# Neighbour codes moved to the one-hots' side by DMA transposes, with a new order of steps, in a two-layer graph kernel

## The chip, the cores and the metric

One NeuronCore of a Trainium2 chip. The metric is the device time of one execution in microseconds (us), as the median of several runs. The engines are TensorE (PE; its weight loads are shown as PEld), VectorE (DVE), ScalarE (ACT) and GpSimd (POOL); SyncE (SP) issues most of the DMAs and does no arithmetic. Each engine has one in-order queue of its own, and the five meet only through semaphores.

## What is computed

```
B, N, C, H = 16, 1024, 64, 128          # x [16,1024,64], adj [16,1024,1024]
h = max(layernorm(x), 0)
x = x + (adj / clip(rowsum(adj), 1)) @ h                          # layer 0
h = max(layernorm(x), 0)
neigh = (adj > 0) off the diagonal;  rank = running count of neighbours in a row
skip  = ceil(n_neighbours / 2) if n_neighbours > 10 else 1
rem   = neighbours whose rank % skip == skip - 1, made symmetric  # thinned out
nd    = what is left, and the node itself
agg[n, c] = 0.25 q25 + 0.5 q50 + 0.25 q75 over h[nd(n), c]        # interpolated quantiles
out = x + (relu((h + agg) @ W1 + b1) @ W2 + b2) * mask
```

The quantiles are the hard part: each node and channel needs a sorted list of its neighbours' values.

## The kernel before, in words

The 16 graphs ("batches") are worked off in 8 pairs, g = 0 to 7, b = 0 and 1.

**Preparation, one batch after another.** For each of 8 row tiles (128 rows) SP loads `ADJ` and, in two halves, its transpose `ADJT`. PE forms the layer-0 messages from `ADJT` (L481). ACT turns `ADJ` into 0/1 neighbours `NEI` (L741, L743), POOL clears the diagonal (`no_loops`, L1270), DVE scans them into running counts in `VR` (`count`, L1045, which first waits until the previous batch's scatter has read that tile of `VR`). POOL works out the thinning of four tiles at a time (L1283 to L1304), ACT and DVE mark the removed neighbours in `RM` (L750, L1051), PE adds up the codes in PSUM (L502 to L511), ACT brings them back as one code per pair of nodes (`coded`, L774) and counts them (`valid`, L779). ACT also ranks the nodes by number of neighbours (L759). POOL then scatters each tile's rows to DRAM, to the place of their rank (`scatter`, L1328). A row of `rows` is 1024 codes, then the node's normalised values h1, x1 and a few counts.

**Lists, one pair at a time.** In rank order the nodes fall into four blocks, `b1` (384 nodes, from 128), `hub` (the 128 with most neighbours), `b2a` (256) and `b2b` (256). The one-hots need the codes with the neighbour on the partitions, so they are transposed: for each of the 16 tiles of a pair SP loads 128 ranked rows into `RR` (L456; two buffers), PE transposes eight 128x128 squares into one of the two PSUM banks `psT` (`positions_up`, L519), ACT copies them to `POSA` or `POSB` (`positions_down`, L790). The tile's h1 is turned too (`turn`, L526) and copied to `Z` (L798). DVE compares `POS` with slot numbers (`one_hots`, L1065, L1068), PE multiplies the one-hots with h1 (`gather`, L560, 14 chunks in two halves), ACT takes the lists out (L861, L866), DVE sorts them (L1086, L1091 for the two smaller kinds; L1132, L1133 with ACT's L884 for the hub), weighs them with coefficients (L1109, L1102, L1138) and adds up (L1150). Two small products, a turn back (L614, L621, L631), the mask (L1157) and POOL's addition (L1354) give the output, which POOL scatters back to node order, 8 indirect DMAs for each of the two batches (`put`, L1362).

**Order.** All steps are laid out in one list, and each engine walks through it taking its own. The list comes from `strands()` (steps of one kind in sequence, one letter each) and `plan()`, which reads the string `ORDER` once for each pair; a letter takes the next step of its strand. `SKEW` says how many steps each strand is ahead: adjacency tiles (`A`, with 16 in a pair) run 24 ahead, that is one and a half pairs. Letters used below: A adjacency tile (ACT, POOL, SP), D scan, T thinning, B and r the removed ones, s and c codes and their count, S scatter of rows, L load of ranked rows, F the transposes through PSUM, d one-hots, m gather, t hub merge (DVE), Q coefficient and weighing, v the two turns of the counts on PE and V the step of POOL ahead of them, E end of a pair, O output scatters. The lead-in before pair 0 can start its one-hots is the same string with the letters of strands that have not begun skipped (`LEAD = 4` passes).

The lines quoted fix the old path's waits: a bank of `psT`, and an area of `POS` that is free when its last gather is done.

```
def positions_up(g, b, rt):                                   # PE
    w.wait_ge(d_row[n % 2], 16 * (n // 2 + 1))
    o = t_free("pos", g, b, rt).bitcast(F16)
    for k in range(T):
        m = e.transpose(o[:, k * P:k * P + P], RR[:, n % 2, k * P:k * P + P], idh)
def positions_down(g, b, rt):                                 # ACT
    w.wait_ge(t_full, u + 1)
    w.wait_ge(p_gm, GATHERED[before])
```

Of the kernel before, what the change touches and what calls it, by code (L numbers as in the profile page):

```python
# [8 lines left out]
ACT = mybir.ActivationFunctionType  # L9
# [15 lines left out]
LEAD = 4  # L25


ORDER = (
    "mRJAssMtQQcNtfJtsQdtFMJtmQtQtdtANetdtQNQQQkmmMMQQdSdQQmQSQaQQmQQcQeLdAMMsFcmssQfQSFSALMdQcDDLMsesSAcdRmS"
    "FMMAVessMMDDTmcSAsQEsDcEdhVSmvFKDMMKdABEBKvdBBmMDMDTdKeFEmRBmeoBEKErBldmrgNFBdKLdrrmFEmrNdeekmdmKdedXEmr"  # L30
    "NrrmeLnQKFstnscssFKAnMsFtMcSsKLFtLScSssdAMtQsscDMdtsDcsSFEAtmMSLMcsAsMSdMEDtEcssSRcSFFADmMMFFtQTtLdFALMM"
    "FmmAeLQFDFQLtdOMMBFFAmFFDBDQQtLdMLFeFmhBrDrFQTMtQtrlBLFFFQQetQrLdBBBBdrtgrrrGOQtmmFsJsGtdctQJsset")

SKEW = {
# [102 lines left out]
def strands():  # L137

    s = {c: [] for c in SKEW}

# [55 lines left out]
    def finish(g):  # L196
# [8 lines left out]
        for b in range(2):  # L205
            add("O", "out", g, b)

    for g in range(NP):
# [3 lines left out]
        for b in range(2):  # L212
            prepare(g, b)
        for blk in BLOCKS:
            fill(g, blk)
# [18 lines left out]
def plan():  # L234

    pl = Plan()
    pl.do("start")
    steps = strands()
    at = {c: SKEW[c] - LEAD * len(steps[c]) // NP for c in SKEW}
    for c in ORDER * (NP + 2 * LEAD):  # L240
        if 0 <= at[c] < len(steps[c]):
            kind, *a = steps[c][at[c]]
            if kind in ("pos", "turn", "dg", "sc", "nvt", "nvr", "flg", "f1", "f2"):
# [38 lines left out]
def program(nc, x_d, adj_d, adjt_d, mask_d, w1_d, b1_d, w2_d, b2_d, cf_d, ch_d, ci_d, cr_d, sel_d, tile_d, row_d, h1_d, out_d):  # L282
    with ExitStack() as ctx:
# [17 lines left out]
        RR = sb("RR", [P, 2, R_X1], F16)  # L301
# [40 lines left out]
        def feat(v, at, w=1):  # L342
# [6 lines left out]
        d_adj, d_adjt, d_row, d_out, d_feat = (  # L349
            [sem(f"{n}{i}") for i in range(2)] for n in ("d_adj", "d_adjt", "d_row", "d_out", "d_feat"))  # L350
# [46 lines left out]
        def positions(g, blk, half):  # L397
# [4 lines left out]
        def turned(g, blk):  # L402
            return positions(g, blk, 0)

        def sync(e):
            w = Once(e)
            for kind, *a in steps:
# [40 lines left out]
                elif kind == "ldr":  # L448
                    g, b, rt = a
                    n = nth["ldr", g, b, rt]  # L450
                    for t in range(T):
                        w.wait_ge(d_sca[t], 16 * (2 * g + b + 1))
                    if n >= 2:
                        w.wait_ge(t_full, t_use("turn", *filled[n - 2]) + 1)
                    n0 = (2 * g + b) * N + rt * P
                    e.dma_start(RR[:, n % 2].bitcast(I32), row_d[n0:n0 + P, 0:R_X1 // 2]).then_inc(d_row[n % 2], 16)  # L456
# [3 lines left out]

        filled = [tuple(s[1:]) for s in steps if s[0] == "ldr"]

        def tensor(e):
# [50 lines left out]
            def positions_up(g, b, rt):  # L514
                n = nth["ldr", g, b, rt]
                w.wait_ge(d_row[n % 2], 16 * (n // 2 + 1))
                o = t_free("pos", g, b, rt).bitcast(F16)
                for k in range(T):
                    m = e.transpose(o[:, k * P:k * P + P], RR[:, n % 2, k * P:k * P + P], idh)  # L519
                m.then_inc(t_full, 1)  # L520
# [960 lines left out]
```

## Time and profile before

| | |
|---|---|
| time, median of 3 runs | 1654.02 us (1653.05 to 1656.76) |
| the profiled execution | 1666.68 us, its span 1664.6 us |
| busy: DVE, PE, ACT, POOL | 1375.1, 1270.5, 1227.5, 775.7 us |
| instructions | 29516 |
| DMA | 233.99 MB, mean 141 GB/s |
| mean granted TensorE clock | 0.878 |

"Busy" is time in which an instruction ran; the rest of the span is the engine's idle time. An idle stretch is put down to what ended it, the releaser. Times are microseconds from the span's start unless marked ns. An engine that is busy for most of a stretch sets its length, and what can still be won there is its idle time.

### The profile page before, as it was taken

How to read it: one execution, taken by the hardware profiler on the slowest of the kernel's cores; microseconds unless marked ns; L12 is line 12 of the kernel's file. 1: busy time of each engine (PE TensorE's matmuls, PEld its weight loads, DVE VectorE, ACT ScalarE, POOL GpSimd, SP SyncE). 2: the span in 40 equal slices, each digit the busy share in tenths (PEclk: the TensorE clock that was granted, in tenths of full speed). 3: DMA queues.
4: the chain of work that ended last, by engine and by line, in shares of the span. 5: the costliest groups of instructions: out<-in, count | busy, mean ns of one | idle time of the engine just before them, and what ended most of it. 6: DMA issues, size and time to landing. Idle time of an engine off the chain costs nothing. (4 is left out here: it accounts for less than half of the span.)

```text
span 1664.6 us, 29516 instructions
## 1 busy us (share of the span) xinstructions
PE 1270.5 (76%) x10929; PEld 847.7 (51%) x10929; DVE 1375.1 (83%) x2557; ACT 1227.5 (74%) x2099; POOL 775.7 (47%) x996
## 2 busy tenths in 40 slices
PE   4675897879888788878888788869888797768642
PEld 3553664556546564556546464556546564444320
DVE  3444459999899898989899898989899898969990
ACT  3687797988788797968788788868788787833310
POOL 0252425271628643383728643383616744631344
PEclk9966598999898898979898998979798898979775
DMA  5464754463536362554536363454526462330100
GB/s 157 139 208 133 235 189 138 149 205 118 171 106 219 113 219 88 172 167 136 182 104 220 112 216 94 163 164 131 197 82 224 124 210 67 109 82 23 30 12 13
DMA packets 139386, 233.99 MB, mean 141 GB/s; under 512 B 62910, under 2 KB 63438, under 8 KB 139224
## 3 DMA queue, kind: packets, MB, share of 16 engines
q1 hardware_dynamic: 124888, 185.54, 36.4%
q0 software_dynamic: 14336, 46.42, 7.4%
q8 instruction: 86, 1.41, 0.4%
q14 instruction: 76, 0.62, 0.1%
HBM read 181.31 MB, written 50.59 MB: 139 GB/s over the span
## 5 line engine op out<-in xcount | busy, mean ns | idle before, releaser
L560 PE MATMUL psG<-OHB,HL 128*64 128x384 f16 (+5 forms) x3584 | 387.4, 361 | 55.1 <-DVE OHB L1065 34.8
L1045 DVE TENSOR_TENSOR_SCAN VR<-NEI 128x1024 f16<-128x1024 f16 x128 | 296.8, 2336 | 125.0 <-POOL NEI L1270 57.3
L481 PE MATMUL psL<-H0A,ADJT 128*128 128x65 f32 x2048 | 311.9, 311 | 65.1 <-DMA ADJT<-in_adjt 37.3
L481 PEld LDWEIGHTS psL<-H0A,ADJT 128*128 128x128 f32 x2048 | 294.7, 224 | 101.7 <-DMA ADJT<-in_adjt 61.2
L560 PEld LDWEIGHTS psG<-OHB,HL 128*64 128x64 f16 x3584 | 213.0, 117 | 195.7 <-DVE OHB L1065 54.0
L1270 POOL TENSOR_TENSOR NEI<-NEI,CH 128x128 f16<-128x128 f16 x128 | 114.1, 894 | 295.8 <-ACT NEI L743 294.5
L1328 POOL DMA_INDIRECT rows<-VR,IDX x128 | 185.4, 1449 | 57.9 <-ACT NEI L779 34.4
L774 ACT ACTIVATE VR<-psT,CF 128x512 f16<-128x512 f32 x256 | 168.5, 681 | 24.6 <-PE psT L511 22.4
L1132 DVE TENSOR_TENSOR HUB<-HUB 128x1472 f32<-128x1472 f32 (+6 forms) x224 | 178.4, 796 | 8.1 <-ACT HUB L884 7.9
L1133 DVE TENSOR_TENSOR HUB<-HUB 128x1472 f32<-128x1472 f32 (+6 forms) x224 | 184.8, 825 | 0.0
L1362 POOL DMA_INDIRECT out<-FR x128 | 162.1, 1266 | 37.5 <-issue 36.9
L884 ACT ACTIVATE HUB<-HUB 128x1472 f32<-128x1472 f32 (+5 forms) x168 | 89.5, 533 | 100.1 <-DVE HUB L1133 98.5
L741 ACT ACTIVATE NEI<-ADJ 128x1024 f16<-128x1024 f32 x128 | 135.1, 1055 | 32.8 <-DMA ADJ<-in_adj 29.6
L750 ACT ACTIVATE RM<-VR,SK 128x1024 f16<-128x1024 f16 x128 | 142.5, 1147 | 16.9 <-POOL SK L1304 16.7
L1065 DVE TENSOR_SCALAR OHB<-POSB 128x512 f16<-128x512 f16 (+2 forms) x544 | 133.0, 313 | 22.9 <-PE psG L560 20.6
L502 PE MATMUL psT<-VR,CH 128*128 128x512 f16 x256 | 104.9, 410 | 59.7 <-ACT VR L774 17.1
L606 PE MATMUL psM<-W,CF 128*128 128x384 f32 (+4 forms) x192 | 84.0, 556 | 78.9 <-DVE W L1109 77.2
L759 ACT ACTIVATE JUNK<-psT,SK 128x1024 int8<-128x1024 f32 x128 | 140.6, 1147 | 0.0
L743 ACT ACTIVATE NEI<-NEI 128x1024 f16<-128x1024 f16 x128 | 135.3, 1057 | 4.1
L779 ACT ACTIVATE NEI<-VR 128x1024 f16<-128x1024 f16 x128 | 135.0, 1055 | 1.3
L1065 DVE TENSOR_SCALAR OHB<-POSA 128x1536 f16<-128x1536 f16 (+6 forms) x320 | 118.2, 427 | 6.6 <-PE psG L560 5.4
L508 PEld LDWEIGHTS psT<-CH,RM 128*128 128x128 f16 x1024 | 86.9, 103 | 64.9 <-issue 14.5
(120 smaller groups left out, 2260.9 us busy)
## 6 DMA issues: line engine op xcount, KB each, us to landing
ADJ<-in_adj SPq DMA_DIRECT2D x128, 512.0 KB
ADJT<-in_adjt SPq DMA_DIRECT2D x256, 256.0 KB
RR<-rows SPq DMA_DIRECT2D x128, 288.0 KB
FR<-rows SPq DMA_DIRECT2D x16, 272.0 KB, 4.0
X<-in_x SPq DMA_DIRECT2D x16, 256.0 KB, 3.5
h<-VR SPq DMA_DIRECT2D x16, 256.0 KB
rows<-VR,IDX POOLq DMA_INDIRECT x128
out<-FR POOLq DMA_INDIRECT x128
```

The lines of the kernel that those rows point to most:

```text
L481: m = e.matmul(ps["L"][:, 65 * (t % 4):65 * (t % 4) + 65], ADJT[:, hf, j, :], H0A[:, T * b + k, :], start=(k == 0), stop=(k == T - 1), ski ...
L560: m = e.matmul(bk[C * b:C * b + C, 0:cols], HL[:, part, (2 * g + b) % 3, k, :], OHB[:, n % 2, b, kk * cols:kk * cols + cols], start=(k == ...
L743: e.activation(nei, nei, ACT.Relu).then_inc(a_nei, 1)
L750: e.activation(RM[:, t, :], VR[:, t, 0:N], ACT.Abs, bias=SK[:, 3, t:t + 1]).then_inc(a_abs, 1)
L759: m = e.activation(JUNK[:, t % 2, :], psT[:, :, :].rearrange("p i c -> p (i c)"), ACT.Sign, bias=SK[:, 5, t:t + 1], accum_out=RS[:, t:t + 1])
L774: e.activation(VR[:, k, 512 * ch:512 * ch + 512], t_bank(u), ACT.Relu, bias=CF[:, CF_LOW:CF_LOW + 1]).then_inc(t_empty, 1)
L1045: e.tensor_tensor_scan(VR[:, t, 0:N], NEI[:, t, 2:N + 2], NEI[:, t, 1:N + 1], 0.0, ALU.add, ALU.add).then_inc(v_cum, 1)
L1065: last = e.tensor_scalar(oh[:, :, at:at + nn], pos, float(2 * d0 - 1), None, ALU.is_equal)
L1132: e.tensor_tensor(b0, a0, a1, ALU.max)
L1133: e.tensor_tensor(b1, a0, a1, ALU.min).then_inc(v_bat, 1)
L1328: e.indirect_dma_start(row_d[:, :], bass.IndirectOffsetOnAxis(ap=IDX[:, gb % 2, t:t + 1], axis=0), VR[:, t, :].bitcast(I32), None).then_in ...
L1362: e.indirect_dma_start(out_d, bass.IndirectOffsetOnAxis(ap=dst, axis=0), fr[:, rt, 0:2 * C].bitcast(F32), None).then_inc(d_out[g % 2], 16)
```

## The change

The path through PE and ACT is taken out for the codes (`positions_up`, `positions_down`, 128 steps each, and `RR`). In its place SP issues one DMA transpose for each block and batch (`ldr`, 64 in all) from DRAM to `POSA` or `POSB`. It waits for the 8 scatters of its batch and until the one-hots that last read this area are made (`v_oh`). Since `RR` also brought h1, a new load `ldh` (letter H, 16 in all) brings h1 of a whole batch to `HR`; `turn` reads it there. DVE's one-hots wait for the DMA's semaphore. `ORDER` is a new string; the lead-in has a string of its own, `LEAD_IN`; strands in it start at 0, others `LATE` steps behind. `put` covers half of the rows of both batches instead of all rows of one.

```diff
-LEAD = 4
 ORDER = (
+    "tJetsscdJstsRQJAmtssQtQdtJtJOOctsmMMNQeHtQAtdNtdtQkQQmmeQcQQQMdHmLQNQffQaQSdQQQQdmMSAMmssQQcMFdSmAVsMhFF"
+    "FFeeQSdcMDDDFdDRSAmsTsMMQcAsKKEdsScKSMMLAssmmDlcDDBMVMdSKAEdBmeBvmvDKTeddoBKMMEmBmBEKedLgBmRdFBErreFrNdk"
+    "QmtmKNddmrmrrrrdNKesesssXnscEtsnKntSsAmFdMMQtsLdctcmdAMEStmSMLEsedADtDcMsMEcAMssMEtSSEscmRtsscADdMtsGMAQ"
+    "QcSFMMetmFSFFQADSQQDQtMMDALQtTQFmQtDDhMTBQBtLBBBlrtdeFtQrrdGBBBrFrLmrMmQrrg")
+LEAD_IN = (
+    "XnnnAMMAMMAMMAMMADDDDTRMMAMBBDBMAMMDADMDTrBBMrBrBrBRNrrrrgNsscsscsAssMcsMAkMMAMNMscSsSAMssMcsDSScRsSADMM"
+    "SADDcTsSsMMAcDSMMADDhDBBrlTBBMMrrBBrRBNrrgXBNNrrknsnscnssAMMScsscAMsSMsADcLMssSMADssScMSMARDDDsscSMMAcDs"
+    "TsMcSMSAMMDBADrBrBBhTLBrrBBBlMMgddrrLrrmm")
+LATE = {"E": 11, "J": 5, "O": 4, "Q": 24, "a": 1, "t": 12}
...
     def fill(g, blk):
+        for b in range(2):
+            add("L", "ldr", g, b, blk)
         for rt in range(r0 // P, (r0 + width) // P):
             for b in range(2):
-                add("L", "ldr", g, b, rt)
-                add("F", "pos", g, b, rt)
                 add("F", "turn", g, b, rt)
...
-        for b in range(2):
-            add("O", "out", g, b)
+        for ch in range(2):
+            add("O", "out", g, ch)
...
-    at = {c: SKEW[c] - LEAD * len(steps[c]) // NP for c in SKEW}
-    for c in ORDER * (NP + 2 * LEAD):
+    at = {c: 0 if c in LEAD_IN else -LATE.get(c, 0) for c in steps}
+    for c in LEAD_IN + ORDER * (NP + 2):
...
+        MADE = {(g, blk): 1 + max(nth["gd", g, c, 1] for c in OF[blk]) for g in range(NP) for blk in OF}
+        LAST = {"b1": (1, "b2a"), "hub": (1, "b2b"), "b2a": (0, "b1"), "b2b": (0, "hub")}
...
+                elif kind == "ldh":
+                    g, b = a
+                    for t in range(T):
+                        w.wait_ge(d_sca[t], 16 * (2 * g + b + 1))
+                    if g:
+                        w.wait_ge(t_full, t_use("turn", g - 1, b, T - 1) + 1)
+                        w.wait_ge(d_hr[b], 16 * g)
+                    n0 = (2 * g + b) * N
+                    e.dma_start(HR[:, b].bitcast(I32), row_d[n0:n0 + N, R_H1 // 2:R_X1 // 2].rearrange(
+                        "(t p) f -> p t f", p=P)).then_inc(d_hr[b], 16)
                 elif kind == "ldr":
+                    g, b, blk = a
+                    area, r0, width = BLOCKS[blk]
                     for t in range(T):
                         w.wait_ge(d_sca[t], 16 * (2 * g + b + 1))
+                    back, last = LAST[blk]
+                    if g >= back:
+                        w.wait_ge(v_oh, MADE[g - back, last])
+                    if g:
+                        w.wait_ge(d_pos[blk][b], 16 * g)
+                    n0 = (2 * g + b) * N + r0
+                    e.dma_start(POS[area][:, b, :, 0:width], row_d.bitcast(F16)[n0:n0 + width, 0:N],
+                                transpose=True).then_inc(d_pos[blk][b], 16)
...
             def turn(g, b, rt):
+                w.wait_ge(d_hr[b], 16 * (g + 1))
                 o = t_free("turn", g, b, rt)
+                e.matmul(o[C * b:C * b + C, 0:P], HR[:, b, rt, :].bitcast(F32), idf, start=True, stop=True).then_inc(
+                    t_full, 1)
...
                     for piece, d0, nd, nn in CHUNKS[c]:
-                        w.wait_ge(t_empty, positions(g, piece, half))
+                        w.wait_ge(d_pos[piece][b], 16 * (g + 1))
...
-            def put(g, b):
-                fr = FR[:, (2 * g + b) % 4]
-                w.wait_ge(o_fin, 2 * (g + 1))
-                for rt in range(T):
+            def put(g, ch):
+                w.wait_ge(o_fin, 2 * g + ch + 1)
+                for b, rt in itertools.product(range(2), range(4 * ch, 4 * ch + 4)):
+                    fr = FR[:, (2 * g + b) % 4]
```

## Rows read from the trace of the kernel before

**Rows 1.** The page, busy time, share of the span and instructions of each engine.

```profile
PE 1270.5 (76%) x10929; PEld 847.7 (51%) x10929; DVE 1375.1 (83%) x2557; ACT 1227.5 (74%) x2099; POOL 775.7 (47%) x996
```

**Rows 2.** Stretches: length, busy PE, PEld, DVE, ACT, POOL; clock, DMA share, GB/s.

```profile
0.00:204.00 204.00, 125.94 (x704) 99.71 (x704) 85.35 (x90) 140.03 (x191) 70.18 (x141) 0.79 0.54 171
204.00:379.00 175.00, 140.99 (x1215) 95.62 (x1216) 147.84 (x266) 149.75 (x245) 75.60 (x106) 0.92 0.54 174
379.00:1319.00 940.00, 771.83 (x6841) 514.96 (x6838) 860.96 (x1597) 764.03 (x1312) 491.79 (x617) 0.90 0.48 154
1319.00:1598.00 279.00, 212.14 (x2021) 128.60 (x2018) 257.16 (x551) 166.87 (x336) 116.82 (x112) 0.91 0.27 83
1598.00:1665.00 67.00, 19.57 (x154) 8.79 (x154) 23.76 (x56) 6.86 (x17) 21.31 (x21) 0.60 0.03 11
```

**Rows 3.** Waits of DVE from 291 to 1458 us: total, times, longest.

```profile
DVE VR L1045 <- POOL NEI L1270: 28.0, 13, 4.8
DVE OHB L1065 <- PE psG L560: 20.1, 6, 4.2
DVE VR L1045 <- issue: 13.9, 4, 4.8
```

**Rows 4.** Timeline near 1100 us, POOL and DVE: start, length, idle before.

```profile
1101.54 2.89 POOL L1362 DMA_INDIRECT out<-FR  x1 [0.16 <-issue]
...
1113.90 0.96 POOL L1362 DMA_INDIRECT out<-FR  x1 [0.30 <-issue]
1114.88 0.45 POOL L1270 TENSOR_TENSOR NEI<-NEI,CH 128x128 f16<-128x128 f16 x1
...
1115.36 2.29 DVE L1045 TENSOR_TENSOR_SCAN VR<-NEI 128x1024 f16<-128x1024 f16 x1 [4.76 <-issue]
```

**Rows 5.** Timeline near 1010 us, PE and DVE.

```profile
1006.17 0.28 PE L530 MATMUL psT<-CF,NV 128*16 128x128 f32 x1 [3.72 <-POOL NV L1336]
...
1016.20 1.71 DVE L1065 TENSOR_SCALAR OHB<-POSB 128x512 f16<-128x512 f16 x8 [3.40 <-PE psG L560]
```

**Rows 6.** Groups by line: busy us, mean ns, idle before.

```profile
L1045 DVE TENSOR_TENSOR_SCAN VR<-NEI 128x1024 f16<-128x1024 f16 x128 | 296.8, 2336 | 125.0 <-POOL NEI L1270 57.3 <-DMA rows<-VR,IDX 53.9 <-issue 13.9
L1133 DVE TENSOR_TENSOR HUB<-HUB 128x1472 f32<-128x1472 f32 (+6 forms) x224 | 184.8, 825 | 0.0
L1132 DVE TENSOR_TENSOR HUB<-HUB 128x1472 f32<-128x1472 f32 (+6 forms) x224 | 178.4, 796 | 8.1 <-ACT HUB L884 7.9
L519 PE MATMUL psT<-CH,RR 128*128 128x128 f16 x1024 | 88.7, 237 | 26.2 <-ACT POSA L790 10.9 <-DMA RR<-rows 4.8 <-ACT VR L774 4.4
L790 ACT ACTIVATE POSA<-psT 128x1024 f16<-128x1024 f16 x80 | 81.8, 1023 | 30.4 <-PE psT L519 21.8 <-PE psT L526 3.7 <-remote 2.6
L790 ACT ACTIVATE POSB<-psT 128x1024 f16<-128x1024 f16 x48 | 48.8, 1017 | 35.3 <-PE psT L519 28.6 <-PE psT L511 6.4
```

**Rows 7.** Around the first one-hot: ACT, POOL, ACT, DVE.

```profile
176.92 1.06 ACT L779 ACTIVATE NEI<-VR 128x1024 f16<-128x1024 f16 x1
178.34 0.98 POOL L1328 DMA_INDIRECT rows<-VR,IDX  x1 [2.11 <-ACT NEI L779]
188.25 1.00 ACT L790 ACTIVATE POSA<-psT 128x1024 f16<-128x1024 f16 x1
204.02 1.96 DVE L1065 TENSOR_SCALAR OHB<-POSA 128x1536 f16<-128x1536 f16 x4 [1.25 <-ACT Z L798]
```

**Rows 8.** DMA issues: KB each, median us from issue to landing.

```profile
FR<-rows SPq DMA_DIRECT2D x16, 272.0 KB, 4.0
X<-in_x SPq DMA_DIRECT2D x16, 256.0 KB, 3.5
```

**Rows 9.** Waits of SP's queue.

```profile
SPq L456 <- PE psT L526: 512.4, 81, 16.1
```

**Rows 10.** End of the run on POOL: the last addition, the last of 16 scatters.

```profile
1637.60 1.26 POOL L1354 TENSOR_TENSOR FR<-FR,HID 128x512 f32<-128x512 f32 x1 [0.23 <-DVE HID L1157]
...
1658.10 0.96 POOL L1362 DMA_INDIRECT out<-FR  x1 [0.30 <-issue]
```

More of the change, by code:

```diff
@@ L137, in strands @@
 def strands():
-    s = {c: [] for c in SKEW}
+    s = {c: [] for c in ORDER}
     def add(c, kind, *args):
@@ L213, in strands @@
             prepare(g, b)
+        for b in range(2):
+            add("H", "ldh", g, b)
         for blk in BLOCKS:
@@ L238, in plan @@
     steps = strands()
-    at = {c: SKEW[c] - LEAD * len(steps[c]) // NP for c in SKEW}
-    for c in ORDER * (NP + 2 * LEAD):
+    at = {c: 0 if c in LEAD_IN else -LATE.get(c, 0) for c in steps}
+    for c in LEAD_IN + ORDER * (NP + 2):
         if 0 <= at[c] < len(steps[c]):
             kind, *a = steps[c][at[c]]
-            if kind in ("pos", "turn", "dg", "sc", "nvt", "nvr", "flg", "f1", "f2"):
+            if kind in ("turn", "dg", "sc", "nvt", "nvr", "flg", "f1", "f2"):
                 pl.use("T", kind, *a)
@@ L348, in program @@
         d_sca = [sem(f"d_sca{t}") for t in range(T)]
-        d_adj, d_adjt, d_row, d_out, d_feat = (
-            [sem(f"{n}{i}") for i in range(2)] for n in ("d_adj", "d_adjt", "d_row", "d_out", "d_feat"))
+        d_adj, d_adjt, d_hr, d_out, d_feat = (
+            [sem(f"{n}{i}") for i in range(2)] for n in ("d_adj", "d_adjt", "d_hr", "d_out", "d_feat"))
+        d_pos = {blk: [sem(f"d_pos_{blk}{i}") for i in range(2)] for blk in BLOCKS}
         CONST = 13 * 16
@@ L395, in m_left, with turned @@
             return {"wz": v_wz, "mk": v_fa}[step[0]], nth[step] + 1
[L397 removed]
+        def turned(g, blk):
             _, r0, width = BLOCKS[blk]
             return max(t_use("turn", g, b, rt) for b in range(2) for rt in range(r0 // P, (r0 + width) // P)) + 1
[L402 to L403 removed]
+        MADE = {(g, blk): 1 + max(nth["gd", g, c, 1] for c in OF[blk]) for g in range(NP) for blk in OF}
+        LAST = {"b1": (1, "b2a"), "hub": (1, "b2b"), "b2a": (0, "b1"), "b2b": (0, "hub")}
         def sync(e):
@@ L459, in sync @@
             w.wait_ge(d_h1, 16 * B)
-        filled = [tuple(s[1:]) for s in steps if s[0] == "ldr"]
         def tensor(e):
@@ L512, in codes @@
                          skip_group_check=True).then_inc(t_full, 1)
[L514 to L520, printed above, removed]
             def turn(g, b, rt):
-                n = nth["ldr", g, b, rt]
+                w.wait_ge(d_hr[b], 16 * (g + 1))
                 o = t_free("turn", g, b, rt)
-                h1 = RR[:, n % 2, R_H1:R_H1 + 2 * C].bitcast(F32)
-                e.matmul(o[C * b:C * b + C, 0:P], h1, idf, start=True, stop=True).then_inc(t_full, 1)
+                e.matmul(o[C * b:C * b + C, 0:P], HR[:, b, rt, :].bitcast(F32), idf, start=True, stop=True).then_inc(
+                    t_full, 1)
             def valid_up(g):
@@ L780, in valid @@
                              accum_out=feat(VR, R_NV)[:, k, :]).then_inc(a_cn, 1)
-            def positions_down(g, b, rt):
-                u = t_use("pos", g, b, rt)
-                blk, = [n for n, (_, r0, width) in BLOCKS.items() if r0 <= rt * P < r0 + width]
-                area, r0, _ = BLOCKS[blk]
-                before = {"b1": (g - 1, "b2a"), "hub": (g - 1, "b2b"), "b2a": (g, "b1"), "b2b": (g, "hub")}[blk]
-                w.wait_ge(t_full, u + 1)
-                if before[0] >= 0:
-                    w.wait_ge(p_gm, GATHERED[before])
-                e.activation(POS[area][:, b, :, rt * P - r0:rt * P - r0 + P],
-                             t_bank(u).bitcast(F16).rearrange("p (k n) -> p k n", n=P), ACT.Copy).then_inc(t_empty, 1)
             def turned_down(g, b, rt):
```

19 lines of the change are left out of this document (2 added, 17 removed), and 3 rows, old and new, of the table SKEW.

## The prediction

> **What bounds the kernel now.** Read the busy times first [rows 1]: DVE is busy 1375.1 us of 1664.6, 83%, ACT and PE some 75%. The average hides the stages, so I cut the span at three landmarks [rows 2]: the first one-hot at 204 us, the first pair's `b1` sum at 379 us, the same sum of the sixth pair at 1319 us, and then the run-out.
> - 0 to 204: DVE is busy 85 of 204 us. Nothing is full. Two batches have to go one after the other through load, scan, removal, codes, scatter, and the first one-hots need both.
> - 379 to 1319: five periods of 188.0 us. DVE is busy 860.96 us, 172.2 a period, so 15.8 us of each are idle. DVE is the bound at 92%; ACT has 152.8 us of work a period and PE 154.4, busy by the modelled ends.
> - 204 to 379: DVE idle 27 us of 175. 1319 to 1598: idle 22 of 279. After 1598: idle 43 of 67, a serial chain.
>
> So work taken off ACT and PE pays nothing by itself in a period. It pays only if one of DVE's 15.8 idle microseconds goes, and no more than these can go: this change leaves all of DVE's instructions in place. The third view is what ended DVE's idle times in the steady part [rows 3]: 28.0 us behind POOL's diagonal clearing, 13.9 us "issue" ahead of the same scan, 20.1 us behind a gather on PE. The timeline explains the two longest kinds. Near 1115 us DVE stands 4.76 us ahead of a scan, because POOL clears the diagonal for it only at 1114.88, and from 1101.54 on POOL has been issuing eight output scatters [rows 4]; the first ones took up to 2.89 us. That pause of 4.75 to 4.76 us is once in every period. Near 1016 us DVE waits 3.40 us for a gather; PE had stood 3.72 us ahead of the counts' turn (L530), which waits for POOL, with the gather queued behind it [rows 5]. That one comes six times, 3.4 us on average.
>
> **The change, part by part.**
> *Codes' old path.* 128 steps with 8 transposes each on PE, 88.7 us of busy time, 11.1 a pair. On ACT 80 + 48 copies, 81.8 + 48.8 = 130.6 us, 16.3 a pair [rows 6]. Both lie beside DVE's work in a period; I cost their removal at nothing there, with DVE's 172.2 as the cover. It gives slack: ACT falls to 136.5 us of 188. It also gives back 16 uses a pair of the two `psT` banks.
>
> *Waits of DVE in a period.* In the old string the first `O` (8 scatters) stands one adjacency tile ahead of a `D`: O M M B F F A m F F D. In the new one both O's stand together, and until the next `D` there are seven one-hot steps (about 1 us each, [rows 7]), five merges (1.62 each, [rows 6]) and a score of Q letters, over 20 us of DVE work. The eight scatters took 13.3 us, 1.67 each [rows 4]; 16 take 20 to 27. I take the 4.75 us out whole. The counts' turn: old V S m v, new V and then t d v v, with the V's themselves further from the loads `f`. I take the 3.4 us out whole as well. Together -8.1 a period. Against this, two O's in one piece hold POOL for that long, in which rows of the batch in preparation can't be scattered and `R`'s additions can't be made. A new pause of at least 1 us seems certain in an order this tight: +1. Net -7 a period, bounds -15.8 (every idle time gone) and +4 (the block meets a scan). Five periods: -35.
>
> *The transposes.* 64 DMAs, 768 KB for b1, 256 KB for the hub, 512 KB for each of b2a and b2b, 33.6 MB in all, where `RR` carried 37.7 MB, and 16 loads of h1 with 4.2 MB: the bytes are equal. No row shows the rate of a DMA transpose. Nearest rows: plain loads with rows of 256 or 272 bytes, 256 KB in 3.5 us and 272 KB in 4.0 us from issue to landing [rows 8], at most 68 to 73 GB/s; and the 174 GB/s that all queues moved together in a stretch [rows 2]. The two b1 transposes of a pair, 1.5 MB, take 9 us at the one and 22 at the other. I take about 13, nearer the stretch, since the loads of rows 8 are mostly the fixed part of a short DMA. The cover: between a pair's last scatter and its first one-hot the new string has four scans (9.3 us), five merges of 1.62 (8.1) and small steps of some 3 us, 20 us of DVE work [rows 6]. With 2 to 3 us until the scatter has landed the b1 transposes end after 16, hidden by 4; at 22 us they would be late by 5 in each pair. b2a and b2b have the six hub chunks as cover. Cost taken: 0; bounds 0 and +5 a pair.
>
> The Trainium skill speaks against the choice of queue: "Advanced Engine Details and Errata", section DGE: Hardware vs Software, lists transposes as worse by the hardware generator, which SP uses, than by the software one. The same page's X-Bar Transpose section has them as fast as plain DMAs, by which nothing in the sum changes. No row here shows either; the first is the rival below.
>
> *SP's queue.* The old loads held it 512.4 us in all for a free `RR` [rows 9], with `ADJ` and `ADJT` queued behind. That wait goes. The new ones are for the scatters, as before, and for one-hots already made, 64 times instead of 128. Behind a transpose stand `A` loads (two buffers) and `H`. Gain: none in a period, where DVE rules; in the lead-in it is part of the next item. If SP needs long to issue a transpose, the next `ADJT` is late: bound +3 a pair.
>
> *Lead-in.* The last code count of pair 0 begins at 176.92 and its scatter at 178.34; the first copy to POSA is at 188.25 and the first one-hot at 204.02 [rows 7]. Those 25.7 us hold six round trips through PSUM, beside scans and removals of batch 2. In the new string 5 B, 5 r, T, one `D` and a tile stand there, 10 to 12 us of work, and the transposes need 2.5 + 13: about 17 us. That is -9. Six or seven copies of 1.02 us go from ACT, whose 140 us in 204 are the most of any engine in this stretch [rows 2]: -6 at most, and I take it. Sum -15, bounds -30 and +5 (the order of the rest is new, and the codes of batch 1 may come later).
>
> *Between.* 204 to 379, idle 27 us: one period's -7, since its output-free POOL gave no 4.75 us pause but much idle behind scatters. 1319 to 1598: the gather pause once, little preparation left: -3. The run-out: 16 scatters of 1.26 us follow the last addition [rows 10]. `put` by halves could begin after the first half's addition, but both O's still stand behind both halves' E steps, and the chain is as long as before: 0.
>
> *Sum.* -15 - 7 - 35 - 3 = -60 against the profiled execution of 1666.68 us: 1606.7. The median is 12.7 us lower than that execution, so 1654.0 - 60 = 1594. **Forecast 1596 us**, about 3.5% less, with 2 us for pauses that I can't name.
>
> **The rivals.**
> (a) *The pauses only move.* The lead-in gains, but DVE still stands 15 us in a period behind other releasers, as it did with an order that had seemed tight. 1654 - 15 - 5 = 1634. For it: 13 of the scans waited for POOL, and POOL's work doesn't shrink. Against: the two repeated pauses have causes that the new string parts.
> (b) *DVE runs full.* The idle time falls to 4 a period: -12 x 5 - 15 - 14 = -89, 1565. For it: ACT and PE now have 50 us of slack each.
> (c) *Slower: b1's transposes land late.* The place is the first one-hot of every pair. The cover is 20 us. If the 1.57 MB take more than 17.5 us (90 GB/s; 2.5 us are the scatter's) DVE waits. The sign turns where that costs 60 / 8 = 7.5 us a pair, at 25 us or 63 GB/s. Half of rows 8's 70 GB/s is 45 us: 27.5 too long, x 8 = 220, less the 60, 1814. A middle case of 35 us gives 1654 - 60 + 8 x 17.5 = 1734, which I take as its time. The skill's "worse" would be this. For it: no row shows the rate, and short rows land slowly. Against: the DMA engines are busy only 0.48 of the time [rows 2].
> (d) *The change moves nothing:* gains of the lead-in are eaten by late transposes. 1654.
>
> **How the numbers follow.** Forecast's case (1580 to 1612) 0.42, (a) 0.20, (b) 0.13, (d) 0.05, (c) 0.20. The range 1560 to 1672 leaves out the far part of (c), 0.13, and the tip of (b). The likeliest case's own range is 1580 to 1612. This kernel's runs spread so that a difference under 0.2% (3 us) can't be told from none. Faster 0.77, the same 0.04, slower 0.19.
>
> **What would show it.** Right: no idle time of 4.7 us ahead of a scan behind output scatters; no 3 to 4 us ahead of one-hots behind the counts' turn; DVE idle under 10 us a period; the first one-hot at or before 190 us; ACT busy near 1097 us, DVE near 1375. Wrong: one-hots that wait for a DMA into POSA, a sign of (c); PE waiting longer for `ADJT`, a sign that transposes hold SP or the DMA engines; periods of 185 us or more, (a). A transposing DMA that also slowed all other traffic would make the whole forecast wrong.

## The result, and the profile after

The changed kernel takes 1789.95 us in the median of 4 runs (1777.02 to 1793.14), against 1654.18 us for the kernel before on the same chip: a ratio of 1.081, interval [1.0761, 1.086]. The forecast was 1596 us. The profiled execution has a span of 1775.2 us against 1664.6: the medians are 135.8 us apart, the two spans 110.6, since the profiled execution of the kernel before was 12.5 us above its median and this one 12.9 us below. The stages below divide up the 110.6.

First the page of the changed kernel, busy time, share and instructions, beside [rows 1]:

```profile
PE 1255.8 (71%) x9905; PEld 811.1 (46%) x9905; DVE 1382.1 (78%) x2557; ACT 1107.8 (62%) x1971; POOL 770.8 (43%) x996
```

The work changed as the prediction had it (ACT 1107.8 us, forecast 1097; DVE 1382.1, forecast 1375). What grew is idle time, DVE's above all. The same stages, cut at the first one-hot and at the `b1` sums of the first, sixth and seventh pair; columns as in [rows 2]:

```profile
0.00:202.00 202.00, 112.33 (x643) 89.99 (x643) 84.86 (x91) 132.21 (x179) 64.31 (x131) 0.82 0.55 170
202.00:392.00 190.00, 141.25 (x1058) 91.20 (x1058) 144.85 (x262) 132.34 (x228) 81.11 (x117) 0.81 0.55 156
392.00:1417.00 1025.00, 764.09 (x6190) 492.53 (x6190) 867.25 (x1596) 688.56 (x1231) 481.13 (x604) 0.83 0.51 142
1417.00:1590.00 173.00, 135.28 (x1126) 83.22 (x1128) 149.74 (x303) 116.08 (x227) 85.89 (x95) 0.87 0.43 116
1590.00:1775.00 185.00, 102.86 (x892) 54.14 (x888) 135.38 (x311) 38.64 (x109) 58.34 (x51) 0.74 0.11 25
```

The first `b1` sum comes 13 us later (392.2 against 379.2). Five periods take 1025 us, 205.0 each, against 187.9: 85 us. The seventh pair adds 9 us and the rest 3; together the 110.6 us between the spans. In a period DVE has 867.25 / 5 = 173.5 us of work (before 172.2) and 31.6 us of idle time (before 15.8). So the loss is idle time of DVE in the steady part, and the next view says what ended it. Waits in that stretch, engine, line, tile, releaser, then total, times and longest; the counterpart is [rows 3]:

```profile
DVE VR L1038 <- DMA rows<-VR,IDX: 45.9, 18, 5.5
DVE OHB L1058 <- PE psG L568: 34.6, 6, 8.4
DVE HUB L1125 <- ACT HUB L879: 31.1, 22, 3.1
DVE OHB L1058 <- issue: 18.2, 4, 5.7
DVE RM L1044 <- ACT RM L756: 9.9, 5, 2.3
DVE OHB L1061 <- PE psG L568: 4.4, 2, 2.8
DVE MARK L1213 <- issue: 4.1, 1, 4.1
...
DVE VR L1038 <- POOL NEI L1263: 0.5, 2, 0.2
...
ACT NEI L747 <- DMA ADJ<-in_adj: 54.1, 10, 9.5
ACT RM L756 <- POOL SK L1297: 50.5, 14, 7.6
...
SPq L269 <- DMA out<-FR: 55.4, 4, 14.0
```

The same view of the kernel before, from 379 to 1319:

```profile
DVE VR L1045 <- POOL NEI L1270: 25.0, 10, 4.8
DVE OHB L1065 <- PE psG L560: 15.9, 5, 4.0
DVE VR L1045 <- DMA rows<-VR,IDX: 10.3, 11, 1.9
...
DVE HUB L1132 <- ACT HUB L884: 2.8, 3, 1.0
...
SPq L267 <- DMA out<-FR: 57.5, 4, 15.5
```

The marks (RM) had 0.6 us there. The pause of [rows 4], scans behind POOL's clearing, did go, as predicted. Five others came or grew in its place. None is a wait for `POSA` or `POSB`: the transposes landed in time.

The fourth of the list has no releaser ("issue"). It stands once in every period where DVE comes to a branch: `overflow` loads a flag, tests it and then writes `MARK` (L1213). First the changed kernel, then the kernel before:

```profile
873.93 0.30 DVE L1058 TENSOR_SCALAR OHB<-POSB 128x512 f16<-128x512 f16 x1 [5.71 <-issue]
...
992.95 0.06 DVE L1220 MEMSET MARK<- 128x1 f32 x1
```

In the five periods these pauses are 18.2 + 4.1 = 22.3 us. In the kernel before no `MARK` of the steady part has a pause ahead of it; there two long scans and the hub's addition stand just ahead of the branch, in the changed kernel short comparisons. That the scans cover the branch is my reading, not shown by a run of its own.

One period's largest pause, of 8.37 us, shows how such a chain is followed. The timeline of the changed kernel, start, length, engine and, in brackets, the idle time before; first the `b1` sums that bound the steady part:

```profile
392.17 0.55 DVE L1143 SCALAR_TENSOR_TENSOR Z<-Z,psM 128x384 f32<-128x384 f32 x1
...
810.99 1.16 POOL L1355 DMA_INDIRECT out<-FR  x1 [0.16 <-issue]
...
831.63 0.96 POOL L1355 DMA_INDIRECT out<-FR  x1 [0.30 <-issue]
...
833.83 1.02 SPq L450 DMA_DIRECT2D FR<-rows  x2
834.89 0.83 SPq L432 DMA_DIRECT2D ADJ<-in_adj  x1
...
840.79 1.06 ACT L747 ACTIVATE NEI<-ADJ 128x1024 f16<-128x1024 f32 x1 [8.93 <-DMA ADJ<-in_adj]
...
841.91 1.97 PE L497 MATMUL psL<-H0A,ADJT 128*128 128x65 f32 x8 [10.25 <-DMA ADJT<-in_adjt]
843.81 2.66 PE L568 MATMUL psG<-OHB,HL 128*64 128x368 f16 x16
...
846.52 1.71 DVE L1058 TENSOR_SCALAR OHB<-POSB 128x512 f16<-128x512 f16 x8 [8.37 <-PE psG L568]
...
1417.24 0.55 DVE L1143 SCALAR_TENSOR_TENSOR Z<-Z,psM 128x384 f32<-128x384 f32 x1
```

POOL issues 16 output scatters in one block, 20.6 us from the first to the last. SP comes to the loads `f` (`FR`, L450), which overwrite rows that output scatters read, and stands until 833.83. `ADJ` and `ADJT` for the preparation are behind it in SP's queue. PE comes to a message step without its `ADJT` and stands 10.25 us with a gather queued behind (L568), and the gather is what DVE's one-hots wait for. The page puts DVE's idle time down to PE; the cause lies further back, in SP's queue and, behind that, in the scatters. The stop itself isn't new: in five periods SP stood 57.5 us for output scatters before and 55.4 us now. New is that the loads behind it come too late: PE waited 15.0 us for `ADJT` before and 51.3 us now.

### The profile page after: what moved, and what is told of

The parts are those of the page before. It is cut to its first block and busy times, and to the rows that moved or that the text cites. A ratio compares the mean times of both kernels' runs of the same rounds, so it can differ in the third digit from the quotient of the medians.

```text
span 1775.2 us, 27210 instructions
## 1 busy us (share of the span) xinstructions
PE 1255.8 (71%) x9905; PEld 811.1 (46%) x9905; DVE 1382.1 (78%) x2557; ACT 1107.8 (62%) x1971; POOL 770.8 (43%) x996
## 5 line engine op out<-in xcount | busy, mean ns | idle before, releaser
L568 PE MATMUL psG<-OHB,HL 128*64 128x384 f16 (+5 forms) x3584 | 424.2, 386 | 76.4 <-DVE OHB L1058 60.9
L497 PE MATMUL psL<-H0A,ADJT 128*128 128x65 f32 x2048 | 319.2, 313 | 139.2 <-DMA ADJT<-in_adjt 92.7
L497 PEld LDWEIGHTS psL<-H0A,ADJT 128*128 128x128 f32 x2048 | 300.8, 226 | 175.3 <-DMA ADJT<-in_adjt 103.8
L568 PEld LDWEIGHTS psG<-OHB,HL 128*64 128x64 f16 x3584 | 224.9, 125 | 239.0 <-DVE OHB L1058 77.5
L1263 POOL TENSOR_TENSOR NEI<-NEI,CH 128x128 f16<-128x128 f16 x128 | 125.9, 983 | 363.1 <-ACT NEI L749 362.2
L1321 POOL DMA_INDIRECT rows<-VR,IDX x128 | 181.1, 1415 | 95.0 <-ACT NEI L785 68.4
L1355 POOL DMA_INDIRECT out<-FR x128 | 137.8, 1077 | 38.0 <-issue 37.7
L614 PE MATMUL psM<-W,CF 128*128 128x384 f32 (+4 forms) x192 | 89.1, 585 | 79.5 <-DVE W L1102 79.5
L518 PE MATMUL psT<-VR,CH 128*128 128x512 f16 x256 | 108.8, 425 | 42.4 <-ACT VR L780 21.9
L1058 DVE TENSOR_SCALAR OHB<-POSA 128x1536 f16<-128x1536 f16 (+6 forms) x320 | 122.5, 437 | 4.2 <-PE psG L568 4.2
```

The lines of the kernel that those rows point to most:

```text
L497: m = e.matmul(ps["L"][:, 65 * (t % 4):65 * (t % 4) + 65], ADJT[:, hf, j, :], H0A[:, T * b + k, :], start=(k == 0), stop=(k == T - 1), ski ...
L568: m = e.matmul(bk[C * b:C * b + C, 0:cols], HL[:, part, (2 * g + b) % 3, k, :], OHB[:, n % 2, b, kk * cols:kk * cols + cols], start=(k == ...
L1058: last = e.tensor_scalar(oh[:, :, at:at + nn], pos, float(2 * d0 - 1), None, ALU.is_equal)
L1321: e.indirect_dma_start(row_d[:, :], bass.IndirectOffsetOnAxis(ap=IDX[:, gb % 2, t:t + 1], axis=0), VR[:, t, :].bitcast(I32), None).then_in ...
L1355: e.indirect_dma_start(out_d, bass.IndirectOffsetOnAxis(ap=dst, axis=0), fr[:, rt, 0:2 * C].bitcast(F32), None).then_inc(d_out[g % 2], 16)
```

## The experiments

Theories at the start: T1, the transposes cost it (they hold SP's queue or slow the other DMAs); T2, the new order of steps costs it.

**1. Plain loads in place of the transposes.** The new order, the same bytes, no transposing:

```diff
-                    e.dma_start(POS[area][:, b, :, 0:width], row_d.bitcast(F16)[n0:n0 + width, 0:N],
-                                transpose=True).then_inc(d_pos[blk][b], 16)
+                    for r in range(width // P):
+                        src = row_d[n0 + r * P:n0 + r * P + P, 0:N // 2].rearrange("p (k f) -> p k f", k=T)
+                        e.dma_start(POS[area][:, b, :, r * P:r * P + P].bitcast(I32), src).then_inc(
+                            d_pos[blk][b], 16)
```

> The changed kernel with each DMA transpose replaced by plain loads of the same rows into the same area, in pieces of 256 bytes (128 in place of 64 instructions; the codes are then not transposed, so the one-hots compare other numbers). Theory T (transposes cost by themselves: SP holds one 1.3 to 5.3 us where a plain load holds it 0.4, 185 us in all, and ADJ and ADJT stand behind): the 54 to 70 us of waits for ADJT and ADJ that were added go, time 1690 to 1730. Theory O (the new order of steps costs, whatever brings the codes): 1770 to 1795, within 1% of the changed kernel.

Measured: 1.0729 [1.0667, 1.079]. Nearly all of the loss is there without a transpose. By the two ratios T1 could own 0.8 of a point in this order; their intervals overlap and allow up to 1.9.

**2. The old order with the transposes.** Old `ORDER` and `SKEW`, old `put`; a block's two transposes at the places of its first two old loads, the h1 load ahead of `b1`'s:

```diff
+                add("L", *(("ldr", g, b, blk) if rt == r0 // P else ("none",)))
+                add("F", "none")
                 add("F", "turn", g, b, rt)
...
+            if kind == "ldr" and a[2] == "b1":
+                pl.do("ldh", *a[:2])
```

> The transposes with the order of before: old string and skews, one transpose for each block and batch at the place of the block's first old load, h1 load ahead of the first, old output scatters, the PE and ACT steps for codes left out. Theory O: the slowdown goes away whole, 1600 to 1660, and ACT's and PE's relief may show as a gain. Theory T: a good part of the slowdown stays, 1700 or more.

Measured: 1.0014 [0.998, 1.0048]. The loss is gone with the order (the string and, with it, the old `put`, the old lead-in and the place of the h1 load).

**3. The new order with the old path.** The kernel before with the new `ORDER`, `LEAD_IN`, `LATE` and `put`; at each `L` all loads, turns and copies of the block in one clump; the copies wait for the one-hots made (`v_oh`), not for the gathers.

```diff
+            if kind == "blk":
+                g, b, blk = a
+                _, r0, width = BLOCKS[blk]
+                for rt in range(r0 // P, (r0 + width) // P):
+                    pl.do("ldr", g, b, rt)
+                    for k in ("pos", "turn"):
+                        pl.use("T", k, g, b, rt)
+                        pl.do(k, g, b, rt)
```

> The new order with the old path: at each new L the block's rows are loaded tile by tile and turned by PE and ACT, h1 with them. Theory O: 1760 or more, since PE and ACT get their 11 and 16 us a pair back in an order laid out without them. Theory T: below the changed kernel, 1680 to 1740.

Measured: 1.1688 [1.1601, 1.1775]. So inside the new order the transposes are worth some 8%, while in the old one they are worth next to nothing. Part of that figure is my clump: DVE waits up to 11.5 us for hub copies of ACT (HUB behind `ACT HUB`, 64.6 us from 500 to 1400), which stand behind it. So the old path's price in the new order is less than these 8%; by how much is not shown.

**4. The old order, transposes late.** In experiment 2 SP stood 162.7 and 79.2 us ahead of transposes for one-hots not yet made. Here a block's transposes stand at its last old loads (the h1 load stays ahead of them):

```diff
-                add("L", *(("ldr", g, b, blk) if rt == r0 // P else ("none",)))
+                add("L", *(("ldr", g, b, blk) if rt == (r0 + width) // P - 1 else ("none",)))
```

> The old order with transposes, each transpose at the place of the block's last old load in place of the first, h1's load ahead. In the kernel with first places SP stood 242 us at transposes that waited for one-hots. If the place of a transpose in SP's queue matters, 5 to 20 us less than the 1670 of that kernel, and so faster than the kernel before. If not: within 5 us.

Measured: 0.9948 [0.9926, 0.997], faster than the kernel before. Waits of SP and DVE in this kernel's whole span:

```profile
SPq L474 <- DVE OHB L1062: 56.4, 2, 32.2
SPq L474 <- DVE OHB L1059: 19.2, 2, 18.4
...
DVE VR L1039 <- POOL NEI L1264: 64.9, 27, 5.4
```

SP's two waits fell to 56.4 and 19.2 us. The scans' wait for POOL (before 57.3, [rows 6]) is still there: moving the transposes doesn't remove it.

**5. The same with plain loads.** Experiment 4 with the edit of experiment 1.

```diff
+                    for r in range(width // P):
+                        src = row_d[n0 + r * P:n0 + r * P + P, 0:N // 2].rearrange("p (k f) -> p k f", k=T)
```

> The old order with late transposes, with plain loads of the same rows in their place (other numbers in the one-hots). If the transposes cost by themselves (2 to 5 us of SP each): 5 to 15 us less than the same order with transposes, 1632 to 1642. If they cost nothing: 1642 to 1652.

Measured: 0.9926 [0.9898, 0.9954]. The intervals overlap, so in this order the transposing itself costs 0.7% at most and may cost nothing. T1 is closed here; in the new order experiment 1 leaves it less than 2 points of the 8.

**6. SP's stop ahead of `f`.** In the changed kernel the two loads `f` move 20 letters later, behind the next adjacency tile:

```diff
-QQQMdHmLQNQffQaQSdQQQQdmMSAMmssQQcMFdSm
+QQQMdHmLQNQQaQSdQQQQdmMSAMffmssQQcMFdSm
```

> The changed kernel with the two f letters (SP's load of the pair's x1 and counts into FR, which waits for the 16 output scatters of two pairs earlier) moved 20 letters down the string, behind the next adjacency tile. Theory F (SP stands 13.9 us at f, the adjacency loads behind it come late, ACT stands 8.9 us, PE 10.3 and DVE 8.4 us, once a period): the 8.4 us go in about six periods, 1735 to 1755 us. Theory G (the lateness has many causes and the next one takes its place): 1775 to 1795.

Measured: 1.0495 [1.0429, 1.0562]; 1.081 before the edit, so some 3 points of the 8. Waits of SP and DVE from 389 to 1386 us, five periods of 199.3:

```profile
DVE VR L1038 <- DMA rows<-VR,IDX: 35.2, 15, 3.9
DVE HUB L1125 <- ACT HUB L879: 32.6, 22, 3.1
DVE OHB L1058 <- issue: 21.1, 4, 6.1
DVE OHB L1061 <- PE psG L568: 11.6, 5, 3.2
DVE RM L1044 <- ACT RM L756: 10.5, 5, 2.3
...
DVE OHB L1058 <- PE psG L568: 2.5, 3, 1.2
...
SPq L269 <- DMA out<-FR: 11.1, 4, 4.0
```

SP's stop fell from 55.4 to 11.1 us and DVE's wait for the gather behind it from 34.6 to 2.5. Part of it came back ahead of the other one-hots (L1061, 4.4 to 11.6), so that both waits together fell from 39.0 to 14.1. The wait for rows fell by 10.7, the others stayed within 7. In the five periods that is 28 us of the 85. This chain is shown.

**7. No output scatters** for pairs 0 to 6, in the changed kernel with `f` in its place; `ldf` waits for the addition instead.

```diff
-            add("O", "out", g, ch)
+            add("O", "out" if g == NP - 1 else "none", g, ch)
...
-                        w.wait_ge(d_out[g % 2], 256 * (g // 2))
+                        w.wait_ge(o_fin, 2 * (g - 1))
```

> The changed kernel with the output scatters of pairs 0 to 6 left out (their outputs aren't written); f then waits only for the additions. It takes away SP's wait and POOL's 20 us block together. If the block of 16 scatters is what the new order pays for: 1650 to 1700. If F is right and POOL's own block costs nothing more: as e5, 1735 to 1755. If neither matters: above 1775.

Measured: 1.0369 [1.0326, 1.0411], periods of 195.0 us. The time, 1715.7 us, lies between the expected ranges: with the scatters' own time gone too, another 1.3 points go, and 3.7 stay without any output scatter in the steady part.

**8. SP's stop at `X`.** In experiment 6 SP also waits 108.0 us in those five periods ahead of the loads `X`. Here `X` is loaded for pair 0 alone.

```diff
-                    if g:
-                        w.wait_ge(o_x1, 4 * g)
-                    for i in range(2):
+                    for i in range(2 if g == 0 else 0):
```

> The changed kernel with f late (1733 us), and x loaded for the first pair alone; later pairs reuse it, so their outputs are of other data. SP then doesn't stand 20 us a period at X for POOL's additions. If SP's second stop costs like the first: 1690 to 1715. If it is covered: 1728 to 1738, and what is left of the slowdown lies in the order of the engines' own steps.

Measured: 1.0482 [1.0431, 1.0533], as without the edit. But SP doesn't stand for less time. In the five periods (387.5 to 1379.5) its wait at the transposes, for one-hots not yet made, grew from 48.8 to 107.6 us, and its wait for a free `ADJT` buffer from 571.7 to 623.9 us: the stop only moved to the next steps of the queue. So the run shows that nothing is won by taking this wait out, not that a stop of that length is free.

**9. `f` moved in the old order.** The first `f` beside the second, in experiment 4's kernel and in the kernel before:

```diff
-mRJAssMtQQcNtfJtsQdt ... QQcQeLdAMMsFcmssQfQSFSALM
+mRJAssMtQQcNtJtsQdt ... QQcQeLdAMMsFcmssQffQSFSALM
```

> The old order with late transposes (1647 us, 0.9948 of before) with its first f letter moved 60 letters down beside the second. In that kernel SP stands 20 us a pair at f for the output scatters, with adjacency loads behind it. If this wait costs there as in the changed kernel: 5 to 30 us less, ratio to before 0.975 to 0.992. If the old order has cover for it (its ACT and PE hardly wait for ADJ): unchanged, ratio 0.993 to 0.997.

> The kernel before with the same move of its first f. SP stands 14 us a period there at f. Same two theories: 0.98 to 0.995 if the wait costs, 0.998 to 1.002 if it is covered.

Measured: 0.9938 [0.9912, 0.9964], which is experiment 4's 0.9948 again, and 1.0017 [0.9987, 1.0046]. There SP stands 87.8 us ahead of `f` in five periods (from 375 to 1312 of experiment 4), more than in the changed kernel, and it is covered too: without it SP waits for free `ADJT` buffers instead (645.3 us in five periods, 561.0 with it).

**10. The kernel before with the first `O` moved** behind the scans and the thinning, the move I had priced at 4.75 us a period:

```diff
-QLtdOMMBFFAmFFDBDQQtLdMLFeFmhBrDrFQTMtQtr
+QLtdMMBFFAmFFDBDQQtLdMLFeFmhBrDrFQTOMtQtr
```

> The kernel before with one letter moved: the first output step O goes from ahead of the scans D to behind them and behind T. If the pause of 4.75 us a period is caused by POOL's eight scatters, as the prediction says, it goes, and the time falls by 10 to 28 us (0.6 to 1.7%). If it only moves to another wait: within 0.3% of before.

Measured: 1.0166 [1.0105, 1.0226], slower, which neither expectation had. The timeline shows the longest of the new pauses:

```profile
963.51 0.69 DVE L985 TENSOR_REDUCE ST<-VR 128x8 f32<-128x512 f32 x1 [7.34 <-POOL VR L1318]
```

The moved scatters now stand together with the other eight, 16 in a row, and hold up POOL's addition for the norms. From 378 to 1330 these pauses are 13.9 us, in four of the periods; the scans still wait 12.8 us for POOL, and 17.1 us of "issue" stand ahead of the hub merges.

**11. The new lead-in ahead of the old order**, with experiment 2's transposes:

```diff
-    at = {c: SKEW[c] - LEAD * len(steps[c]) // NP for c in SKEW}
-    for c in ORDER * (NP + 2 * LEAD):
+    lead = first + "L" + second + "L" + third + "LLLLL" + rest + "F" * 13 + "sscssde"
+    at = {c: 0 if c in lead else SKEW[c] for c in SKEW}
+    for c in lead + ORDER * (NP + 2):
```

> The old order with transposes behind the new lead-in (its letters, then F x13 and s s c s s d e to reach the old skews). The lead-in's own share: the first b1 sum came at 392 us in the changed kernel and at 378 with the old order and transposes. If the new lead-in costs that: 1680 to 1690. If it gains the 15 us of the prediction: 1650 to 1660.

Measured: 1.0117 [1.0092, 1.0143] against experiment 2's 1.0014, between the two expected ranges. About one point by the ratios; by the traces the first `b1` sum comes at 384.1 us instead of 378.3 and the span is 1.4 us longer, so that 0.3 to 1 point is what can be said. It had to be fitted to the old string with 13 `F` and seven more letters, so even that isn't wholly the lead-in's own. In the changed kernel's lead-in two lines are worth a look, a scan that waits twice as long for rows as before and the first one-hot, 2 us earlier than in [rows 7], not 14:

```profile
97.47 2.38 DVE L1038 TENSOR_TENSOR_SCAN VR<-NEI 128x1024 f16<-128x1024 f16 x1 [28.63 <-DMA rows<-VR,IDX]
...
201.95 2.00 DVE L1058 TENSOR_SCALAR OHB<-POSA 128x1536 f16<-128x1536 f16 x4
```

The long wait is a trap: the same scan waited 13.64 us before and began at 96.83, so it is 0.6 us later, and DVE only had less to do ahead of it. The time is lost further on: the last code count of pair 0 begins at 187.72 (before 176.92), its last scatter at 193.25 (178.34).

**12. Single places, or a pause that only moves?** With `f` moved, periods still took 199.3 us. ACT stood 58.5 us in five of them ahead of the marks (RM, letter B) for POOL's thinning (T), with the hub copies behind it; nothing like that is in the kernel before. Scans (D) stood 35.2 us behind the previous batch's scatter of their tile (S). Three kernels; the first has B later and `f` moved, the second also two D (one of them with its T, R and two K), the third B alone in the changed kernel:

```diff
-TeddoBKMMEmBmBEKedLgBmRd ... TBQBtLBBBlrtdeFtQrrdG
+TeddoBKMMEmmEKeBdBLgBmRd ... TQtLlBBtBBdBerFtQrrdG
```

The second kernel has these besides:

```diff
-QSdcMDDDFdDRSAmsTsMMQcAsKKEds ... ADtDcMsMEcAMssMEtSS
+QSdcMDDDFdSAmsKKDRTsMMQcAsEds ... ADtcMsMEcAMssMEtDSS
```

> The changed kernel with the loads f moved as in the run before (1.0495 [1.0429, 1.0562] to the kernel before) and in addition B letters moved: behind the last T of the string TBQBtLBBBl... becomes TQtLlBBtBBdB..., and behind the second one EmBmBEKe becomes EmmEKeBdB. In the trace of the run with f moved ACT stands 58.5 us in five periods ahead of marking (RM) for POOL's thinning, where the kernel before has none of it; its copies for the hub merges are queued behind, and DVE waits 32.6 us for those and 10.5 us for RM (before: 2.8 and 0.6). Theory 1 (what is left of the loss is a step placed where its input is late, so that it holds others on its engine; B behind T is the largest such place): ACT's wait for POOL's thinning falls below 25 us in five periods, DVE's two waits together below 20 us, periods 195 us instead of 199, ratio 1.025 to 1.038. Theory 2 (as when O was moved in the kernel before: the pauses only move, and what is left belongs to the order as a whole): ACT's wait falls as well but DVE's idle time stays within 2 us of 26.5 a period, ratio 1.044 to 1.055.

> As the run beside it with the B letters moved, and the scans D moved too that follow their tile's scatter too closely: DDDFdDRSAmsTsMMQcAsKKE becomes DDDFdSAmsKKDRTsMMQcAsE, and ADtDcMsMEcAMssMEtSS becomes ADtcMsMEcAMssMEtDSS. In the trace with f moved DVE waits 35.2 us in five periods for the scatters of the previous batch ahead of scans (10.3 in the kernel before), 3.4 to 3.9 us at each of these two places in every period. Theory 1 (single places): that wait falls below 15 us, periods 2 to 4 us shorter than beside it, ratio 0.01 to 0.02 lower than that of the run beside it. Theory 2 (pauses only move): the wait falls but others grow (results and thinning R and T come later, and with them the marks), ratio within 0.006 of the run beside it or higher.

> The changed kernel with the B letters alone moved (f stays where it is). If the places act independently of each other, the gain is the same as between the run with f moved alone and the one with f and B moved (Theory 1: 1.081 becomes 1.057 to 1.070). If the stop of SP behind the output scatters is the longer chain of the period, so that slack won on ACT is lost there, the ratio stays within 1.076 to 1.086. By Theory 2 it stays there as well, or rises.

Measured, first: 1.0456 [1.0428, 1.0484], periods of 196.7 us. DVE's two waits are 18.4 and 18.1 us, together 36.5 instead of 43.1, and ACT's wait is 45.3: the move was too short, and the marks that came later were waited for themselves. Its interval overlaps the one without the edit and lies in the range of the second theory; at most 1.3 points.

Second: 1.0298 [1.0281, 1.0315], 1.6 points below the first, periods of 194.8 us. The stretch and DVE's waits from 384 to 1361:

```profile
384.00:1361.00 977.00, 763.78 (x6190) 489.79 (x6190) 869.33 (x1602) 692.08 (x1233) 475.10 (x607) 0.84 0.53 149
```

```profile
DVE VR L1038 <- DMA rows<-VR,IDX: 27.7, 17, 5.3
DVE HUB L1125 <- ACT HUB L879: 17.8, 15, 3.4
DVE RM L1044 <- ACT RM L756: 16.9, 20, 1.8
DVE W L1079 <- ACT Z L793: 12.3, 5, 2.9
DVE OHB L1058 <- issue: 10.5, 4, 2.8
```

The wait for rows fell from the first kernel's 39.8 to 27.7 us (not below 15), and the "issue" pauses ahead of one-hots from 18.4 to 10.5, which I had not aimed at. But a wait of 12.3 us for ACT's `Z` is new, once a period: in five periods rows and "issue" gave 20.0 us, and DVE's idle time fell from 115.2 to 107.7. So a single place can be mended here, and a good part of its pause does come back elsewhere. (The two profiled executions are only 4.2 us apart, one at the fast end of its kernel's runs, the other at the slow end; the 1.6 points come from all runs.)

Third: 1.0762 [1.0738, 1.0785], and five periods of 205.9 us where the changed kernel has 205.0. Its interval overlaps 1.081's. With SP's stop in place the move buys nothing that can be told: DVE's wait for hub copies fell from 31.1 to 18.7 us, and that for marks grew from 9.9 to 20.4.

## Why the prediction was wrong

The loss, in the order in which it was taken away. Of 8.1 points, some 3 go with SP's stop ahead of `f` (experiment 6), about 2 more with the places of B and D together (12); B's alone, without the first, gave nothing that can be told. The other three stay: in the second kernel of experiment 12 five periods still lose 35 us, the first sum 5 and the end 12. Between 0.3 and 1 point of them may be the lead-in's (11); the rest is open. The waits in that kernel (rows 27.7, hub copies 17.8, marks 16.9, `Z` 12.3, the branch 13.4) suggest more places of the same kind, but this was not tried.

By the prediction's steps:

- *What bounds the kernel.* Right: DVE's idle time is what moves. ACT's work fell by 120 us, and in the old order that gave 0.5%; in the new one the relief is worth up to 8% (experiment 3).
- *Codes' old path, transposes.* Right. Cost taken 0; the transposes of the changed kernel landed 6.6 and 4.1 us after issue in the median, no one-hot waited for one from 392 to 1417, and experiments 4 and 5 can't be told apart. My 13 us for two `b1` transposes stand well beside that.
- *Waits of DVE in a period: -7.* This is the step that failed. Its minus terms are real. The scans' wait for POOL fell from 25.0 to 0.5 us, and two more pauses of [rows 4]'s kind, 4.76 us each, which the view had under "issue", went too. PE's wait ahead of the counts' turn, 20.2 us in five periods, is gone from its list. The term that failed is the "+1" for new pauses "in an order this tight". The same view, after less before, gives +35.6 for rows, +18.7 for gathers, +28.3 for hub copies, +9.3 for marks, against -24.5 for POOL: together 67.4. The "issue" pauses add 8.4 (22.3 at the branch against 13.9, of which 9.5 were POOL's) and small ones the rest of 78.7, or 15.7 us more idle time a period, where I had 7 less. I had followed two pauses of the old string into the new one and had not asked what the new one puts too close together. The string could have been read for part of it: both `O` in one piece ahead of `f`, a D nine letters behind its tile's S (18 at least in the old one), a B eight to eleven letters behind its T in three of four places (in one of four in the old one).
- *SP's queue: "Gain: none in a period".* The bound +3 was for transposes. I named who stands behind a transpose and not who stands behind `f`, which waits for output scatters. Its stop was as long in the old order, and covered there; what uncovers it in the new one is not shown.
- *The two O's in one piece.* I priced the block as POOL's time alone (20 to 27 us; 21.6 measured from first issue to last end) and left out who else waits for those scatters. Experiment 10 also shows that the -4.75 could not be had by that move alone.
- *Lead-in: -15.* The first one-hot came 2 us earlier, at 202, not 190. The tail behind the last scatter got shorter, more than I had it (8.7 us, from 25.7), but that scatter comes 14.9 us later.
- *Between: -7 up to the first `b1` sum, -3 from the sixth sum on.* These failed like the periods: 15 us more (190 against 175) and 14 us more up to the eighth sum (289.8 against 275.6).
- *Run-out: 0.* Right: from the eighth sum to the end 68.2 us against 70.1.

Of the rivals, (c) had the sign and, by chance, the nearest time (1734, and 1814 for its far case, against 1790), but not the mechanism: it had the transposes late. (a), pauses that move, came nearest to the mechanism, but as a smaller gain (1634), with no gain in a period as its worst. A range whose upper end rested on one mechanism had no room for an order that is worse by itself. What the Trainium skill says in "Advanced Engine Details and Errata", section DGE: Hardware vs Software, that transposes do worse by the hardware generator, changed no time that could be measured here. The same page's X-Bar Transpose section has them as fast as plain DMAs. Experiments 4 and 5 agree with that for the kernel's time, within their 0.7%; they don't measure the rate of a transpose.

The best version is the kernel before with transposes at late places: 0.9948, or 0.9938 with `f` moved, which can't be told apart.

## What to carry to other kernels

When steps are reordered, go through each in-order queue and ask of every step that waits for something moved what stands behind it, down to the engine that bounds: here SP's queue carried a stall from POOL's scatters to ACT, PE and DVE. Price the new order's own tight places (a consumer within a few microseconds behind its producer) with the same care as the pauses that it removes. And test an order and a mechanism apart before they are put together: here the mechanism was worth half a percent in the old order, and the order that came with it cost eight. Then look whether a stop that was taken out only moved to the next step of its queue.

## What the runs showed of the hardware

A DMA transpose holds SP's queue far longer than a plain load. All transposes of the changed kernel, duration at SP as min, median and max in ns:

```profile
L473 SPq DMA_TRANSPOSE POSA<-rows x32: 1861/3546/5309, 162.5 to 1618.1; - x32
L473 SPq DMA_TRANSPOSE POSB<-rows x32: 1278/2168/2985, 200.8 to 1660.3; - x32
```

A load of `RR` took 328 ns in the median of the kernel before. Over a pair that is some 23 us of SP's time, covered here; whether a kernel with a fuller queue covers it, no run shows.

Some of POOL's smallest instructions took five to nine times as long while DVE scanned. The timeline of experiment 6, POOL's thinning beside two scans:

```profile
969.69 2.08 POOL L1281 TENSOR_SCALAR SK<-SK 128x4 f32<-128x4 f32 x1
...
972.02 2.25 POOL L1284 TENSOR_SCALAR SK<-SK 128x4 f32<-128x4 f32 x1
...
969.47 2.28 DVE L1038 TENSOR_TENSOR_SCAN VR<-NEI 128x1024 f16<-128x1024 f16 x1
971.97 2.29 DVE L1038 TENSOR_TENSOR_SCAN VR<-NEI 128x1024 f16<-128x1024 f16 x1 [0.22 <-DMA rows<-VR,IDX]
```

Each of the two long ones ends with the scan beside it; in the chain right behind, with no scan beside it, the same two lines take 0.23 and 0.46 us. The first chain takes 9.6 us (968.15 to 977.8), the second 5.8: part of why B stood too close behind T.

DVE's idle time at its branch is 3.05 to 5.71 us in each of the five steady periods of the changed kernel. In those of the kernel before there is none ahead of `MARK`, and once 3.26 us behind it. In the second kernel of experiment 12, where the hub's addition stands right ahead of the branch, it is 2.55 to 2.88 us.

TensorE's granted clock in the steady part was 0.90 before [rows 2], 0.86 in the old order with transposes (375 to 1312) and 0.83 after; PE was busy 82%, 80% and 75% of these stretches. Taking work off PE did not let the rest of it run at a higher clock; all three are means over stretches at either of its two levels, 1.2 and 2.4 GHz. The lower clock explains little of the loss: PE's busy time for the same work is 764.1 us in the changed kernel's stretch and 751.4 in experiment 4's, 12.7 us apart, where the stretches are 88 us apart.
